# Softmax sums of the third attention: taken by VectorE straight from the exponentials, without GpSimd's two folds

## What is computed

```python
# A: self attention in windows of 128 rows, 16 heads of 16 channels
x = x + self_attn(ln(x) * (1 + sc) + sh) * gate
# B: attention over 77 context rows, of whose scores each row keeps the 16 largest per head
x = x + topk_cross_attn(ln(x) * (1 + sc) + sh, context) * gate
# C: SwiGLU with a hidden width of 1024
x = x + (silu(a) * b @ w_m2 + b_m2) * gate
# D: plain attention over the same 77 context rows, the third attention
scores = einsum('bqhd,bkhd->bhqk', q, k) / sqrt(16)
attn   = softmax(scores, axis=-1)          # 16 heads x 77 scores per row
out    = x + (attn @ v) @ Wp + bp
```

## Time and profile before

| | |
|---|---|
| Median of 3 runs | 1026.23 us (1023.97 to 1029.4) |
| Profiled execution, its own time | 1025.22 us |
| Its span | 1023.4 us |
| TensorE busy | 975.6 us, 95% |
| VectorE busy | 843.6 us, 82% |
| ScalarE busy | 779.4 us, 76% |
| GpSimd busy | 697.2 us, 68% |
| Granted TensorE clock, mean | 0.984 |
| Chain that ended last | TensorE 87%, VectorE 4%, ScalarE 2%, GpSimd 2% |

### The profile page before, as it was taken

How to read it: one execution, slowest core, us unless ns; L and a number is a source line. 1 busy time by engine, 2 the same in 40 slices (tenths; PEclk the granted TensorE clock), 3 DMA queues, 4 the chain that set the end, 5 groups by cost and what they waited for, 6 DMA issues and landing times.

```text
span 1023.4 us, 33174 instructions
## 1 busy us (share of the span) xinstructions
PE 975.6 (95%) x10980; PEld 863.1 (84%) x10980; DVE 843.6 (82%) x4240; ACT 779.4 (76%) x1679; POOL 697.2 (68%) x1093
## 2 busy tenths in 40 slices
PE   5886999999999999999999999999999999999996
PEld 5574788899988889899888888889998988988884
DVE  2348999988998898888898898888999889889644
ACT  2234778788888888888888888888888888887764
POOL 1048556877777777777777777777777777766853
PEclk9887999999999999999999999999999999999999
DMA  8064000000000000000000000000000000000000
GB/s 299 14 143 67 7 8 1 13 12 13 12 13 12 13 7 8 12 13 12 13 13 12 13 11 4 13 12 12 12 12 13 12 13 8 7 7 8 7 7 17
DMA packets 33993, 23.15 MB, mean 23 GB/s; under 512 B 22995, under 2 KB 31443, under 8 KB 33184
## 3 DMA queue, kind: packets, MB, share of 16 engines
q1 hardware_dynamic: 33824, 21.02, 8.1%
HBM read 16.19 MB, written 4.83 MB: 21 GB/s over the span
## 4 chain that ended last, share of the span: by engine, by line
PE 87%; DVE 4%; issue 3%; ACT 2%; POOL 2%; DMA 1%; SPq 0%; POOLq 0%; DVEq 0%; ACTq 0%
PE ps L2137 21%; PE ps L2148 10%; PE ps L2013 8%; PE ps L2126 8%; PE ps L2115 7%; PE ps L2099 7%; PE ps L2085 4%; PE ps L2044 3%; PE ps L2061 3%; PE ps L2024 3%; PE ps L2074 3%; PE ps L2002 2%; PE ps L2034 2%; PE ps L1943 2%; PE ps L1973 1%
## 5 line engine op out<-in xcount | busy, mean ns | idle before, releaser
L2137 PE MATMUL ps<-hT_C,w_m_sb 128*128 128x128 f32 x2048 | 250.4, 276 | 0.4 <-ACT pT_B L859 0.3
L2137 PEld LDWEIGHTS ps<-hT_C,w_m_sb 128*128 128x128 f32 x2048 | 241.2, 192 | 3.7 <-issue 1.4
L866 ACT ACTIVATE silu_C<-ps,cols_sb 128x128 f32<-128x128 f32 x256 | 91.1, 367 | 74.4 <-PE ps L2137 73.0
L2148 PE MATMUL ps<-w_m_sb,hidden_C 128*128 128x256 f32 x512 | 120.7, 379 | 0.0
L538 POOL TENSOR_TENSOR p_B<-p_B,rc_B 128x616 f32<-128x616 f32 x64 | 77.7, 1216 | 62.0 <-DVE p_B L1401 61.0
L1393 DVE MATCH_REPLACE8 scores_left_B<-mx_B,scores_left_B 128x77 f32<-128x77 f32 x512 | 108.3, 224 | 0.0
L1389 DVE MATCH_REPLACE8 scores_left_B<-mx_B,scores_B 128x77 f32<-128x77 f32 x512 | 107.8, 224 | 0.0
L2148 PEld LDWEIGHTS ps<-w_m_sb,hidden_C 128*128 128x128 f32 x512 | 94.6, 190 | 11.4
L1483 DVE SCALAR_TENSOR_TENSOR hidden_C<-ps,cols_sb,silu_C 128x128 f32<-128x128 f32 x256 | 85.2, 343 | 22.6 <-ACT silu_C L866 22.4
L538 POOL TENSOR_TENSOR p_D<-scores_D,rc_D 128x616 f32<-128x616 f32 x63 | 77.0, 1225 | 27.8 <-DVE rc_D L1438 26.9
L1341 DVE TENSOR_REDUCE mx_A<-ps 128x8 f32<-128x1024 f32 x64 | 75.3, 1218 | 17.1 <-PE ps L2044 17.1
(11 more groups left out here) (186 smaller groups left out, 2582.9 us busy)
## 6 DMA issues: line engine op xcount, KB each, us to landing
x_A<-in_x SPq DMA_DIRECT2D x64, 64.0 KB, 2.2
out<-y_D SPq DMA_DIRECT2D x64, 64.0 KB, 2.1
w_m_sb<-in_w_m SPq DMA_DIRECT2D x3, 1024.0 KB, 5.8
w_mod_sb<-in_w_mod SPq DMA_DIRECT2D x2, 1024.0 KB, 11.4
w_qkv_sb<-in_w_qkv SPq DMA_DIRECT2D x1, 768.0 KB, 6.9
w_gate_sb<-in_w_gate SPq DMA_DIRECT2D x1, 768.0 KB, 7.4
rows_sb<-in_rows SPq DMA_DIRECT2D x1, 768.0 KB, 8.7
w_mod_sb<-in_w_mod SPq DMA_DIRECT2D x1, 512.0 KB, 4.1
```

The lines of the kernel that those rows point to most:

```text
L866: sc.activation(SA[:, j, :], bank(f"C.up{j}")[:, 0:P], ACT.Silu, bias=col("bm1_a", j)).then_inc(sa_ok, 1)
L2137: ins = mm(bank(f"C.up{j}")[:, half * P:(half + 1) * P], w_m1[:, k, m:m + P], HT["C"][:, t % HT_COPIES["C"], k, :], start=(k == 0), stop=( ...
L2148: ins = mm(bank("C.dn0")[:, 0:CH], G[:, t % G_COPIES, j, :], w_m2[:, j, :], start=(j == 0), stop=(j == HJ - 1))
```

## The change

`row_sums` reads the exponentials of all 77 columns of the 16 heads from S["D"] in one instruction, for the tiles 0 to 29. It waits for the exponentials' semaphore instead of the folds'. `fold_sums`, its calls in all of GpSimd's rounds, its semaphore and its two buffers are gone. The output tile y_D lies where the second fold buffer was; so the buffers allocated behind it move a little. The order of all other instructions, on every engine, is the same.

```diff
-        FOLD = [None, sb("fold2_D", [P, HEADS, LCP // 4])]
+        Y = sb("y_D", [P, CH])
...
-        FOLD[0] = sb("fold_D", [P, HEADS, LCP // 2])
-        Y = sb("y_D", [P, CH])
...
-            def fold_sums(t):
-                pool.wait_ge(e_ok["D"], KC * t + KC)
-                if not first(t):
-                    pool.wait_ge(rc_ok["D"], 2 * t)
-                n = LCP // 2
-                g.tensor_tensor(FOLD[0][:], S["D"][:, :, 0:n], S["D"][:, :, n:2 * n], ALU.add).then_inc(fold_ok, 1)
-                n = LCP // 4
-                pool.wait_ge(fold_ok, 2 * t + 1)
-                g.tensor_tensor(FOLD[1][:], FOLD[0][:, :, 0:n], FOLD[0][:, :, n:2 * n], ALU.add).then_inc(fold_ok, 1)
...
             def body(i):
...
                 run(normalise_weights, i, 3, "B", 1)
-                run(fold_sums, i, 6)
                 run(less_max, i, 2, "B", 0)
                 run(normalise_weights, i, 6, "D", 0)
...
                 else:
-                    dve.wait_ge(fold_ok, 2 * t + 2)
-                    src = FOLD[1][:]
+                    dve.wait_ge(e_ok["D"], KC * t + KC)
+                    src = S["D"][:, :, 0:LC]
                 v.tensor_reduce(DS[s][:, :, 0], src, AX.X, ALU.add).then_inc(rc_ok[s], 1)
```

More of the change, by code:

```diff
@@ L222, in block_kernel @@
         sum_last, rc_last, n_last = (sem(n) for n in ("sum_last", "rc_last", "n_last"))
-        keep_ok, t16_ok, e16_ok, mxd_ok, fold_ok = (sem(n) for n in ("keep_ok", "t16_ok", "e16_ok", "mxd_ok", "fold_ok"))
+        keep_ok, t16_ok, e16_ok, mxd_ok = (sem(n) for n in ("keep_ok", "t16_ok", "e16_ok", "mxd_ok"))
         u_ps, sa_ok, g_ok = sem("u_ps"), sem("sa_ok"), sem("g_ok")
@@ L615, in fill @@
                 normalise_weights(3, "B", 1)
-                fold_sums(0)
                 normalise_weights(0, "D", 0)
@@ L637, in fill @@
                 normalise_weights(4, "B", 1)
-                fold_sums(1)
                 less_max(5, "B", 0)
@@ L681, in drain @@
                 add_bias(TILES - 2, "B")
-                fold_sums(TILES - 6)
                 normalise_weights(TILES - 6, "D", 0)
@@ L696, in drain @@
                 less_max(TILES - 5, "D", 1)
-                fold_sums(TILES - 5)
                 less_max(TILES - 1, "B", 0)
@@ L713, in drain @@
                 add_bias(TILES - 4, "D")
-                fold_sums(TILES - 4)
                 normalise_weights(TILES - 4, "D", 0)
@@ L723, in drain @@
                 reciprocal_root(TILES - 2, "D")
-                fold_sums(TILES - 3)
                 normalise_weights(TILES - 3, "D", 0)
```

## The result

Five runs of the changed kernel gave a median of 1034.2 us (1030.93 to 1037.15), five of the kernel before 1026.23 us (1023.97 to 1029.4). The ratio is 1.007 with a 95% interval of 1.0041 to 1.0098: slower by 0.7%. The profiled execution took 1034.4 us, span 1032.6, which is 9.2 more than the span of the one before. A second set of runs of the same kernel is told with the experiments.

A forecast was written before the change was run, and what follows sets the result against it. TensorE was taken to bound steady rounds. Steady losses of 7.9 us plus 1.8 in drain and fill (0.95 + 0.55 + 0.3) made 9.7 on the profiled 1025.22: 1034.9, said as 1035, range 1029.5 to 1041.

The forecast's parts named there:

- The sum of 1232 elements: VectorE's sum for 30 tiles: 1.42 us instead of 469 ns, so +0.95 us per tile (0.32 to 1.07).
- Where the delay is absorbed: VectorE behind the sum: idle time ahead of ev_A takes up 0.20 us, everything from there on is 0.75 late.
- The slack at up3: TensorE's up3 weights load behind VectorE's hidden 0: 0.44 us slack, so 0.31 us lost per steady tile.
- That it doesn't pile up: VectorE's 0.54 us idle ahead of hidden 3 shrinks the 0.75 delay to TensorE's own 0.31 each round.
- Tiles 1 to 26: Steady pattern: 25 x 0.31 = 7.8 us, with 0.1 for t = 25 makes 7.9 lost.
- Tile 27: Last rounds, sum straight to hidden 0 and up3's load: no slack, the whole 0.95 us is lost.
- Tile 28: Last rounds, p_D feeding TensorE's transposes: sum starts up to 0.2 earlier, p_D about 0.73 late, 0.55 us lost.
- Tile 29: Last rounds: no wait of TensorE found behind the sum, nothing lost.
- Tile 0: First rounds: 0.61 us idle at hidden 1 leaves 0.35 for x_C and up4; 0.3 us taken as lost.
- A: Slack at up3 wider than read, 0.66 us: a tile loses 0.09, time 1029 to 1030; 16%.
- B: Folds had slowed VectorE, so steady rounds lose nothing: 1025 to 1028 us; 5%, 1% more for a gain over 0.5%.
- C: Stall costs more than its length, by pile-up, added waits or a 1.54 us sum: 0.5 per tile, 1039.5 us; 20%.

The follow-up runs named there:

- experiment 3: Changed kernel with VectorE's sum over only 16x60 = 960 elements of a weight buffer; loss per tile 0.00, span 1030.7 us.
- experiment 4: Changed kernel with one more VectorE sum of 616 elements right behind the reciprocal for tiles 1 to 29; 1054.98 us, 0.97 lost per tile.
- experiment 2: Kernel before with the sum over 1232 elements straight from the exponentials, GpSimd's folds kept but unread; 1034.55 us, 0.27 lost per tile.
- experiment 1: Changed kernel, folds gone, with VectorE's sum over only 320 elements of a weight buffer; 1024.21 us against 1024.74 for the kernel before.
- 5: Changed kernel with half the heads summed earlier in the round, last rounds' sums moved too; median 1028.23 us against 1025.24, ratio 1.0025.
- experiment 7: Kernel before plus an unused 864-element VectorE sum per tile where VectorE stood idle waiting for TensorE's down; 1030.73 us, loss per tile 0.00.
- 8: Changed kernel with the split sums of 5, but tiles 1, 2 and 26 keep the whole sum at its old place; 1029.67 us against 1026.61, ratio 1.002.
- 6: Changed kernel with only the last rounds' moves: tile 27's sum split around x_C, tile 28's ahead of x_C; 1034.62 us.

## Why the prediction was right

Predicted were 1035 us and +9.7 on the profiled execution; measured 1034.2, and +9.2.

- **The sum of 1232 elements**: predicted 1.42 us, measured 1.418. The slope between 320 and 616 elements by itself gives 1.40, and for 960 elements 1.12 where experiment 3 measured 1.142; that the rounding went up was luck of 0.02. The estimate by the formula of the Trainium skill, VectorE: DVE Perf Modes, section "The TRN2 errata — SBUF-src ops pay a fixed extra latency per instruction", 1.34 us, is 0.08 short here, and the section itself says that the formula gives too little.
- **Where the delay is absorbed**: predicted 0.20 at ev_A, so hidden 0 0.75 late. From the sum's start to hidden 0's end it was 4.89 us before and is 5.61 now: 0.72 late, 0.23 absorbed.
- **The slack at up3**: predicted 0.44 with a restart of 0.12, so 0.31 lost per tile. Measured restart 0.12, loss 0.27, which is 0.72 - 0.44 to a hundredth; the term was 0.04 too large through the 0.20. Experiments 3 and 4 show the shape: +0.67 costs 0, +0.95 costs 0.27, 0.69 more costs 0.70 more.
- **That it doesn't pile up**: shown by the equal periods, and by the idle time at hidden 3, 0.17 where about 0.1 was said.
- **Tiles 1 to 26**: predicted 7.9, measured 7.16, of which 0.35 is tile 10's idle moment; without it the rounds lost 6.8. **Tile 27**: 0.95 and 0.95. **Tile 28**: p_D starts at 982.11; less the 7.42 that it was late already, that is 0.72 behind the place of the earlier trace rows, where 0.73 was said; 0.55 predicted, 0.53 lost. **Tile 29**: 0 and 0. **Tile 0**: 0.3 and 0.22. The 0.2 by which the fold had held up the old sum is real: the new one starts at 980.25, less 7.42 that is 0.22 ahead of the old one's 973.05. In experiment 2 the sum doesn't wait for the fold either, and it lost the same 0.54.
- **Foreseen by no step**: 0.91 us won ahead of the first changed instruction, 0.35 lost at tile 10, and 1.25 lost to the clock at the end. The first and the last nearly cancel, and that is luck: the 9.2 look nearer to the 9.7 than what they are made of. From tile 0 to tile 29 the loss was 8.86, and 8.5 of it by the predicted mechanism.
- **The rivals.** A wanted a restart of nothing and 0.09 a tile: the restart is 0.12. B, the other side, fell with experiments 1 and 2. C wanted 0.5 a tile: the sum stayed at 1.418, up2's wait is part of up3's, and the delay doesn't pile up, as the equal periods and experiment 4's one for one show.

What the experiments missed were whole times, in 3, 5, 7 and 8 and by a little in 4: each was reckoned from the kernel before's span plus steady losses, as if the fill and the clock were the same in each execution.

## What to carry to other kernels

A helper engine that is far from being the bound can be shielding a nearly full one: what GpSimd's 2.4 us bought was 0.95 us of VectorE ahead of the instructions that hand PSUM banks back to TensorE. Price such an edit by the distance from the release to the waiter's start, less the restart, at the first place behind it; add to it what an idle moment on the way absorbs (here 0.44 and 0.23). Within that room the edit costs nothing, above it the excess is paid in full in every round, and so is each small idle moment that the room used to swallow (tile 10). A small loss of this kind doesn't show in the busy share of the bound engine (0.27 a tile), a large one only in part (0.97). Compare periods and running differences rather than spans where less than 1% is at stake, and check the first and last rounds on their own: they have other room than the steady ones.

## What the runs showed of the hardware that was not expected

The granted clock of TensorE fell to 0.5, its lower level, in the middle of work in some kernels, for 3.4 us and twice for 6.8 (the ends of experiments 3 and 8), at 173 to 181 us (experiments 3, 4, 5 and 7; about 1.6 us each) and at 1005 to 1018 us, 1034 in experiment 4 (the changed kernel both times and experiments 2 to 6 and 8; 1.2 to 2.3 us). The kernel before, experiment 1 and experiment 7 kept it at 1.00 until behind their last matmuls or nearly so (1021.4, 1020.5, 1027.4). At the end the traces divide by what tile 27 lost: 0.43 us or more against the kernel before in all that fell, at most 0.24 in the three that did not. That is a coincidence in eleven traces and no cause shown; nothing was run that changes only that. About 1.25 of the 9.2 us hang on it, and whether they belong to the change stays open.
